# A two-layer decoder on one core: identity products between the shared attention's scores and sums, and scores on 64 rows instead of 48

## What is computed

```python
# layer 1, the second attention, and how the layers are strung together
q = (x @ Wq + bq).reshape(1, B * N, H, hd)
kv = (cond @ Wkv + bkv).reshape(1, -1, 2, H, hd)
k, v = (kv[:, :, 0], kv[:, :, 1])
...
q = _fq_sym(q, axis=-1)
k = _fq_sym(k, axis=-1)
v = _fq_sym(v, axis=2)
attn = jnp.einsum('bhqd,bhkd->bhqk', q, k)
attn = jax.nn.softmax(attn.astype(jnp.float32), axis=-1)
attn = _fq_unsigned(attn, axis=-1)
out = jnp.einsum('bhqk,bhkd->bhqd', attn, v)
...
x = _layernorm(x + _L1_attn_ref(...), axis=-1)
x = _layernorm(x + _L1_xattn_ref(x, ctx_2048, ...), axis=-1)
x = _layernorm(x + _L1_ffn_ref(...), axis=-1)
```

## Time and profile before

| what | value |
|---|---|
| median of 3 runs | 1417.25 us (1414.0 to 1420.13) |
| the profiled execution | 1417.26 us |
| its span, first to last instruction | 1415.5 us |
| mean granted TensorE clock | 0.907 |
| PE busy | 1237.8 us (87%), 9,108 products |
| DVE busy | 1046.5 us (74%) |
| ACT busy | 675.3 us (48%) |
| POOL busy | 135.1 us (10%) |
| DMA | 86.06 MB, mean 61 GB/s |

### The profile page before, as it was taken

The page is one execution under the profiler, slowest core; times in us unless marked ns, Lnnn a source line. Parts: engine busy times, 40 slices in busy tenths (PEclk is TensorE's granted clock), DMA queues, the critical chain, the costliest instruction groups (busy, mean ns, idle before and its releaser), DMA issues.

```text
span 1415.5 us, 24455 instructions
## 1 busy us (share of the span) xinstructions
PE 1237.8 (87%) x9108; PEld 850.1 (60%) x9113; DVE 1046.5 (74%) x2349; ACT 675.3 (48%) x1286; POOL 135.1 (10%) x223
## 2 busy tenths in 40 slices
PE   6979999999999999999899999989899746677686
PEld 3747666766766766766676676656777623333344
DVE  6778578588677767858857775744888788889877
ACT  2336435434533633643553363442444358878751
POOL 2210010010011001002001100000000011111101
PEclk9989999999999999999999999999999955555588
DMA  7331002000100200200010013000300179989910
GB/s 240 154 105 63 12 12 66 13 1 16 63 12 16 62 12 12 66 12 5 26 49 12 12 63 120 20 23 24 78 8 9 31 124 167 173 151 181 166 23 30
DMA packets 176117, 86.06 MB, mean 61 GB/s; under 512 B 138240, under 2 KB 170368, under 8 KB 175744
## 3 DMA queue, kind: packets, MB, share of 16 engines
q1 hardware_dynamic: 174848, 84.13, 25.3%
q10 hardware_dynamic: 1152, 0.36, 0.1%
HBM read 43.57 MB, written 5.24 MB: 34 GB/s over the span
## 4 chain that ended last, share of the span: by engine, by line
PE 63%; DVE 19%; ACT 6%; issue 6%; DMA 5%; POOL 1%; SPq 0%; DVEq 0%; POOLq 0%; ACTq 0%
PE ps_t L1890 12%; PE ps_p L1874 11%; PE ps_s L2123 8%; PE ps_o L2040 5%; DMA w_moe<-w_moe 4%; PE ps_o L2030 4%; PE ps_o L1955 4%; PE ps_o L2123 3%; PE ps_p L1932 3%; DVE probs L1275 2%; ACT w_moe L1116 2%; PE ps_s L1932 2%; PE ps_o L1959 2%; DVE w_moe L1778 2%; DVE row_max L1281 1%
## 5 line engine op out<-in xcount | busy, mean ns | idle before, releaser
L1890 PE MATMUL ps_t<-ident,probs 128*128 128x128 f32 x1072 | 170.3, 280 | 28.5 <-ACT probs L1065 8.0
L925 ACT ACTIVATE probs<-probs 128x512 f32<-128x512 f32 x184 | 115.6, 628 | 136.6 <-DVE probs L1275 136.6
L1890 PEld LDWEIGHTS ps_t<-ident,probs 128*128 128x128 f32 x1072 | 123.2, 142 | 78.1 <-issue 37.9
L887 ACT ACTIVATE probsT<-ps_t 128x512 f32<-128x512 f32 x232 | 136.5, 589 | 64.0 <-PE ps_t L1890 63.8
L2123 PE MATMUL ps_s<-w_moe,xbT 128*128 128x352 f32 x352 | 122.1, 471 | 0.0
L1874 PE MATMUL ps_p<-w_qkv,xinT 128*128 128x512 f32 (+1 forms) x240 | 104.8, 560 | 11.4 <-DMA xinT<-in_xT 7.6
L2399 PEld LDWEIGHTS ps_p<-vals,w_moe 128*128 128x128 f16 x1024 | 37.2, 105 | 97.7 <-DMA w_moe<-w_moe 76.4
L831 POOL TENSOR_TENSOR rms<-mean_sq,neg_half 128x8 f32<-128x8 f32 x40 | 67.1, 1679 | 267.3 <-DVE mean_sq L1309 267.3
L887 ACT ACTIVATE bigT<-ps_t 128x512 f32<-128x512 f32 (+1 forms) x128 | 69.0, 553 | 33.3 <-PE ps_t L1890 31.4
L2399 PE MATMUL ps_p<-vals,w_moe 128*128 128x16 f16 x1024 | 48.2, 176 | 38.6 <-DMA w_moe<-w_moe 37.9
L2123 PEld LDWEIGHTS ps_s<-w_moe,xbT 128*128 128x128 f32 x352 | 64.0, 194 | 22.1 <-issue 1.5
(11 more groups left out here) (342 smaller groups left out, 2736.5 us busy)
## 6 DMA issues: line engine op xcount, KB each, us to landing
w_out<-in_wT_out SPq DMA_DIRECT2D x8, 2048.0 KB, 8.4
w_moe<-in_wT_gu SPq DMA_DIRECT2D x1, 5632.0 KB, 17.6
w_moe<-in_wT_down SPq DMA_DIRECT2D x1, 2816.0 KB, 10.2
keys<-keys2T SPq DMA_DIRECT2D x8, 256.0 KB, 2.0
keys2T<-keys SPq DMA_DIRECT2D x4, 512.0 KB, 10.4
w_moe<-w_moe SPq DMA_TRANSPOSE x128, 3.3
w_qkv<-in_wT_qkv SPq DMA_DIRECT2D x3, 512.0 KB, 4.9
w_qkv<-in_wT_qkv SPq DMA_DIRECT2D x1, 1536.0 KB, 8.3
```

Of the source, the lines that this page charges most:

```text
L887: nc.scalar.activation(dst, src.bitcast(BF16) if dst.dtype == BF16 else src, ACT.Copy)\
L925: nc.scalar.activation(probs[:, at % 4, :], probs[:, at % 4, :], ACT.Exp).then_inc(L0.exped, 1)
L1890: ins = nc.tensor.transpose(dst[:, i * P:(i + 1) * P], src(i), ident_b[:] if bf else ident[:])
```

## The change

Three things change, all in PE's program. DVE's, ACT's, POOL's and SP's instructions stay as they are, in the same order.

1. The score products of the shared attention contract the full block of 64 rows instead of 48. The 16 added rows are zeros in the stacks of queries and keys.
2. In each head of the shared attention four products of the identity, 256 columns each, are put ahead of the wait for the head's transposition. They write columns 256 to 511 of the bank in which the sums are formed; the sums use columns 0 to 255.
3. At the end of causal attention, `dense` with 11 products of 512 columns stands in three places: at the end of the step in which tile 7 gets its sums, before the wait for tile 7's norm, and at the end of that step.

```diff
+IDLE_FILL = 11
...
                 if p is not None:
                     project(L1, ("v1", p), lane_of(p).xinT, w_qkv1, 2 * D, D)
+                if q == LAST:
+                    dense(ps_s[:, 1, :], IDLE_FILL)
                 if q is not None:
                     pe.wait_ge(N4.x_ready, q + 1)
...
                 if s is not None:
                     causal_sums(s, 1)
+                if LAST in (s, q):
+
+                    dense(ps_s[:, 1, :], IDLE_FILL)
...
                     for n in range(2):
-                        r = slice(STK * n, STK * n + 3 * HD1)
+
+                        r = slice(STK * n, STK * n + STK)
                         ins = nc.tensor.matmul(psum[:, n, :], (own if h % 2 == n else other)[r, h // 2, :],
...
+                    for n in range(4):
+
+                        nc.tensor.matmul(ps_p[:, av % 2, D:2 * D].rearrange("p (a b) -> p a b", a=2), ident_b[:],
+                                         ident_b[:].unsqueeze(1).broadcast_to([P, 2, P]), start=True, stop=True)
                     pe.wait_ge(turned2[v % TURNS], 16 * (v // TURNS) + 16)
                     for n in range(TILES):
```

## The result

The changed kernel takes 1413.25 us (median of 20 runs, 1410.56 to 1417.18), the kernel before, run beside it, 1417.78 us (20 runs). The ratio is 0.9967, with a 95% interval of 0.9961 to 0.9974. That is 4.5 us faster, where 10.7 us had been forecast: less than half. The direction was right, and 1413.25 lies inside the range of 1396 to 1424, but the gain clears the noise without clearing half a per cent. Times of whole executions are medians of those in the chip's faster state; one execution of `rows48` (1642.19 us) and one of `lag7` (1430.95 us) fell in a slower one and are left out.

The account below looks back on a forecast made before the run. In the shared attention DMA, DVE and ACT, not PE, were taken as busiest. Gains of 2.0 (causal attention's end), 8.4 (shared heads) and 0.3 us (stage end) made 10.7, from 1417.2 to 1406.5 us; range 1396 to 1424.

Parts of the forecast that it names:

- (b): End of causal attention: three batches of 2.6 us fit into PE's waits for DVE and keep the clock full; 2.0 us gained.
- (a): Shared scores on 64 rows instead of 48: costed at nothing, could use more of the array.
- (d): Shared heads: clock taken as held with short falls; 8.4 us gained, 1.2 us a tile for seven tiles.
- (c): Four identity products a head: hidden by the DMA wait or DVE, nothing at full clock; without cover up to 1.4 us a tile.
- The landings: Shared heads: 59 us of DMA landings on the chain, 29.3% of 200 us, get 3% longer and give back 1.8 us.
- PE's crossings: Shared heads' chain: projections gain 6.4 us (1.91 to 1.0 each), scores 3.8, sums 1.0; together 11.2 us.
- (e): End of the shared stage, first feed-forward block: 0.3 us gained, since the last transposition hardly lands before the block ends.
- rival 1: Shared stage: the clock swings and low parts cost more than high ones give; 1433 us at half low; chance 0.16.
- the formula: Rival 1's sum for share x of eight tiles low: -2.3 - 8.4(1 - x) + 44x, zero at x = 0.20.
- Rival 2: Shared tiles: DMA takes the gain back through longer landings, only 2 to 6 us stay; 1413 us; chance 0.17.
- Rival 4: Shared stage: clock low for about a fifth, gains and losses cancel; 1417 us; chance 0.07.
- Rival 3: Shared tiles: waits on PE kept DVE idle, so DVE becomes the bound at 23 us a tile; 1394 us; chance 0.10.

Follow-up runs that it names:

- rows48: The changed kernel with the shared scores back on 48 rows; 1417.58 us, ratio 0.9997 to the kernel before.
- lag7: start_five with the sums seven heads behind the scores instead of five and eight transposition buffers instead of six; 1403.01 us, ratio 0.9917 to the kernel before.
- start: The changed kernel with six identity products of 256 columns also in each of the first five shared heads; 1410.16 us, ratio 0.9961 to the kernel before.
- start_five: start with five identity products a head instead of four; 1408.46 us, ratio 0.9944 to the kernel before.
- not_project: start_five without the five products in each tile's one head whose sums stand right ahead of the output projection; 1410.16 us, ratio 0.9940 to the kernel before.
- lag6: start_five with the sums six heads behind the scores instead of five and seven transposition buffers instead of six; 1403.80 us, ratio 0.9892 to the kernel before.
- not_late: The changed kernel without the four products in heads 11, 12 and 13 of each tile; 1416.03 us, ratio 0.9991 to the kernel before.

## Why the prediction was wrong, point by point

**Causal attention's end, (b): right.** 1.8 us for a forecast of 2.0. The batches took 2.54 us each (2.6 had been forecast), the waits behind them ended later than the batches, and the clock held to 1142. The first batch and the wait left behind it, and the first projection, to be laid beside the earlier trace rows:

```profile
1126.31 2.54 PE L1901 MATMUL ps_s<-ident_b 128*128 128x512 bf16 x11
...
1129.63 0.44 PE L1892 MATMUL ps_t<-ident,kdup 128*128 128x128 f32 x2 [0.79 <-DVE kdup L1680]
...
1130.55 1.13 PE L1876 MATMUL ps_p<-w_qkv,kdup 128*128 128x256 f32 x4
...
1131.51 2.54 PE L1901 MATMUL ps_s<-ident_b 128*128 128x512 bf16 x11
...
1134.67 0.44 PE L1892 MATMUL ps_t<-ident,w_moe 128*128 128x128 f32 x2 [0.62 <-DVE w_moe L1658]
```

**The 64 rows, (a): right in cost, undersold in effect.** They cost nothing, and without them the change gave nothing.

**The heads: the step that failed is (d), "I take it as held with short falls".** The sum has no term for the falls. In the profile the clock fell for 17.1 us from 1142.4, since the products hang on the sums and the first five heads have none (with products there, in `start`, this fall lasted 3.4 us), and then six times for 3.4 us. Together 35 of 195.5 us ran at 0.50. What this cost can be read tile by tile. A tile here goes from its first reduction to the next tile's (the eighth to its last), and the differences are of starts that are not rounded:

| tile | 1 | 2 | 3 | 4 | 5 | 6 | 7 | 8 |
|---|---|---|---|---|---|---|---|---|
| before, us | 22.7 | 26.3 | 26.1 | 25.5 | 25.1 | 25.3 | 25.4 | 23.9 |
| changed, us | 24.0 | 24.1 | 24.9 | 25.8 | 24.2 | 24.1 | 24.2 | 24.3 |
| gain, us | -1.3 | 2.1 | 1.2 | -0.3 | 1.0 | 1.2 | 1.2 | -0.4 |
| of it at 0.50, changed, us | 15.0 | 3.4 | 3.4 | 3.4 | 3.4 | 0 | 0 | 6.8 |

The forecast was nothing for the first tile and 1.2 us for each of the others. In the two tiles without a fall just that came. The first reductions of the sixth and of the eighth tile, in the kernel before and then in the changed one, and then the changed kernel's stretch between them (clock 1.00) and its chain of waits:

```profile
1270.30 1.21 DVE L1778 TENSOR_REDUCE w_moe<-ps_t 128x1 f32<-128x1024 f32 x1
...
1321.06 1.21 DVE L1778 TENSOR_REDUCE w_moe<-ps_o 128x1 f32<-128x1024 f32 x1
```

```profile
1267.53 1.22 DVE L1780 TENSOR_REDUCE w_moe<-ps_t 128x1 f32<-128x1024 f32 x1
...
1315.80 1.22 DVE L1780 TENSOR_REDUCE w_moe<-ps_o 128x1 f32<-128x1024 f32 x1
```

```profile
1268.00:1316.00 48.00, 40.10 (x464) 24.35 (x464) 43.95 (x57) 40.54 (x69) 9.70 (x34) 1.00 1.09 178
...
by line: DVE w_moe L1780 19.5%; issue 19.2%; DMA w_moe<-w_moe 16.5%; ACT w_moe L1118 15.4%; PE ps_p L2349 4.0%; PE ps_p L2411 2.7%; POOL w_moe L864 2.5%; PE ps_p L2407 2.3%; PE ps_s L2393 2.1%; DVE w_moe L1748 1.8%; DVE w_moe L1650 1.8%; DV
```

The first tile, with 15 of its 24 us at 0.50, took 1.3 us more instead of nothing, and tiles 2 to 8 gained 6.1 us instead of 8.4. One tile of one profile is weak evidence: in the three kernels with low clock the first tile differs by up to 1.2 us and another by up to 0.8. But in `start`, `start_five` and `not_project` six more tiles passed without a fall, and they took 0.6 to 1.4 us less than the same tiles before. And with most of the falls gone `start_five` gained 6.9 us over the kernel before. What a fall costs is uneven: the fourth tile lost with 3.4 us at 0.50 and the second gained most with as much; 20 us less at 0.50 went with 6.0 us between `rows48` and the changed kernel, with 2.2 between that and `start_five`.

Three terms stand beside it. *The products' cover, (c):* "I cost them at nothing at full clock" was nearly right for full clock: in the two tiles above the products (L2407) have 2.3% of the chain, 0.6 us a tile, where (c) had named 1.4 as the most. At low clock they are dear. From 1316 to 1340, where the clock fell twice, they have 18.4% of the chain:

```profile
by line: DMA w_moe<-w_moe 20.0%; PE ps_p L2407 18.4%; issue 15.2%; DVE w_moe L1780 14.7%; PE ps_p L2411 5.9%; PE ps_t L2393 4.6%; PE ps_s L2393 4.5%; PE ps_o L2393 4.3%; PE ps_p L2349 4.0%; DVE xa L1649 1.8%; DVE w_moe L1650 1.8%; ACT w_moe
```

(d) had worked out 1.71 us of PE for a head at low clock. That is what came: where PE doesn't wait, the sums start 1.71 us apart at 0.50, and 1.05 us apart once the clock is full.

```profile
1155.69 0.40 PE L2411 MATMUL ps_p<-vals,w_moe 128*128 128x16 f16 x8
...
1157.40 0.40 PE L2411 MATMUL ps_p<-vals,w_moe 128*128 128x16 f16 x8
...
1160.23 0.35 PE L2411 MATMUL ps_p<-vals,w_moe 128*128 128x16 f16 x8
...
1161.28 0.35 PE L2411 MATMUL ps_p<-vals,w_moe 128*128 128x16 f16 x8
```

*The landings:* I priced a rise of 3% for them. The median landing from 1160 to 1330 was 3.3 us before and 3.4 us after, so the size was about right; the 5.33 us shown above was a long one. What the prediction missed is that their share of the chain (29.3%) could be taken away: one more head of lag was worth 7.6 us without the change and 8.7 with it. That was not among my rivals, but it is not what made this forecast fail either, by the 5.8 and 4.8 us above.

*PE's crossings:* scores took 0.39 us and the projection 0.97 us on the chain instead of 1.91, as forecast.

Of the missing 3.6 us `start_five` brings back 2.2. Whether its remaining falls or its fifth product keep the rest can't be said from these runs: no kernel has the full clock without the products.

**The end, (e): right in this profile, not in general.** 0.3 us came in the profiled execution. But from the last shared reduction to the end, the three kernels without any added identity product took 70.4 to 70.6 us, and the fourteen with them 70.0 to 74.2, with a median of 71.7. If the changed kernel usually loses these 1.2 us too, -1.8 and -4.8 make -5.4 us, which is nearer to the measured -4.5; its one profile doesn't show it. In `start_five`, with 72.1 us, the stretch from 1338 to 1346 was granted 0.79. What lengthens this part was not tested.

**The rivals.** The swinging clock (rival 1) was there in kind: nine falls after 1140. But it cost less than I had priced. At a share of 18% low the formula gave 1.3 us of gain, and the three parts gave 6.9. What the 44 us of its formula left out is PE's waits for landings, 34.8 us of them in 180, which longer products can fill; that reason was not tested by itself. Rival 2's time, 1413 us, is the measured one, and that is chance: landings hardly got longer, and `lag6` moved 178 GB/s over the stage where the changed kernel moved 171. Rival 4 had the share of low clock nearly right (a fifth), but its 1417 us came out of the same formula. Rival 3 (DVE as the bound at 1394 us) comes near once the lag is six: DVE is busy 22.55 of 24 us in the row of `lag6`.

The page of the Trainium skill that rival 1 rested on, "TensorE: Matmul & The Clock Gate", in "A second HAM failure mode: psum-queue depth-cycling", tells of a clock that goes up and down where PE idles briefly between groups of products. The trace agrees: the grant over the stage was 0.91 in the changed kernel and 0.87 in `rows48`, made of full and half pieces.

The prediction held the same page's rule on idle gaps between bursts, in "Why this matters for your kernels", against the trace, because the clock stayed low over the whole stage. That was read too quickly. The rule names what brings a full clock down, and in the kernel before the clock fell at 1126.9, inside PE's wait of 3.15 us. The trace goes beyond the rule in the changed kernel, where the clock fell six times after 1160 while PE's longest wait up to 1340 was 1.8 us.

## What to carry to other kernels

When a chain of waits has a DMA landing in it again and again, ask first how many steps of lag the consumer gives that landing; another buffer and one more step of lag may be worth more than any engine on the chain (7.6 us here for a change of two numbers, against 4.8 for the clock). A gain from the clock needs a price for its falls: four products a head that only keep the clock up were nearly free while it was full and dear while it was low (2.3% against 18.4% of the chain here). They need a place directly ahead of a wait (ahead of the landing rather than behind the sums was worth 5.4 us). They need it from the first round on too, also where the work they hang on has not begun; here the first tile lost 1.3 us without them. And a change that is measured with and without another one tells whether they touch: the lag gave 7.6 and 8.7 us, the change 4.8 and 5.8, so they are two gains and not one.

## What the runs showed of the hardware

- The clock over the heads depended on things that look small: 48 or 64 rows of two products (0.87 or 0.91 from 1146 to 1336), and three heads of sixteen without products (0.83). Rows of zeros counted for it: the 16 added rows hold nothing else.
- A product of 256 columns took 0.15 us at full clock in groups of four (0.61 us for four, from first start to last end) and 0.26 at half (1.04 us for four).
- DMA's transpositions reached 182 GB/s over a tile of `lag6`, and its busy share 1.13 there, against 184 GB/s in the tile around 1160 before.

The first of these can be seen in one row of `not_late`, and the second in two rows of the changed kernel's timeline:

```profile
1146.00:1336.00 190.00, 156.46 (x1630) 91.38 (x1631) 163.58 (x198) 154.49 (x261) 36.43 (x127) 0.83 0.99 167
```

```profile
1150.43 1.04 PE L2407 MATMUL ps_p<-ident_b 128*128 128x256 bf16 x4
...
1163.18 0.61 PE L2407 MATMUL ps_p<-ident_b 128*128 128x256 bf16 x4
```
